# Attention over 32 heads: values two tiles at a time, six tiles of each head's softmax sum added by DMAs, the context normalised a head later

## What is computed

```python
xn = layernorm(x)
qkv = xn @ qkvw + qkvb                       # 32 heads of 32 columns each
scores = einsum('bhqd,bhkd->bhqk', q, k) / sqrt(32)
probs = softmax(scores)                      # rows of 2048 keys
ctx = einsum('bhqk,bhkd->bhqd', probs, v)
attn = ctx @ ow + ob
gate = softmax of the 16 best router scores of 64 experts, zero elsewhere
z = (xn @ A_w.T) * gate                      # 64 experts of rank 8
out = x + attn + (z @ B_w.T) * 2
```

## Time and profile before

| | |
|---|---|
| median of three runs | 2847.87 us |
| the profiled execution | 2850.67 us |
| its span in the trace | 2848.9 us |
| TensorE busy (matmul) | 2751.8 us, 97% |
| VectorE busy | 1637.0 us, 57% |
| ScalarE busy | 1289.9 us, 45% |
| GpSimd busy | 1733.5 us, 61% |
| mean granted TensorE clock | 0.98 |

### The profile page before, as it was taken

One profiled execution on the slowest core, in us unless ns is written; L12 is line 12 of the kernel. 1 busy time (PEld: TensorE's weight loads), 2 busy tenths in 40 slices (PEclk: granted clock), 3 DMA queues, 4 the chain that ended last, 5 costly groups with the idle time before them and its releaser, 6 DMA issues. The chain is left out here.

```text
span 2848.9 us, 36121 instructions
## 1 busy us (share of the span) xinstructions
PE 2751.8 (97%) x13776; PEld 1612.5 (57%) x13776; DVE 1637.0 (57%) x2553; ACT 1289.9 (45%) x2299; POOL 1733.5 (61%) x406
## 2 busy tenths in 40 slices
PE   7999999999799999999999999999999999997999
PEld 6888887778444444444444444444444444436887
DVE  8411111111778777777777778777877787724221
ACT  3111111110066666666666666666666666672100
POOL 0111111110199989898999899889989998982121
PEclk9999999999599999999999999999999999998999
DMA  4233333112611121112111211221122111004432
GB/s 140 98 129 112 110 110 111 66 66 89 162 27 38 38 60 34 38 38 60 35 41 35 60 35 42 45 50 38 38 51 44 38 38 35 9 16 144 128 103 92
DMA packets 145852, 188.56 MB, mean 66 GB/s; under 512 B 87152, under 2 KB 112240, under 8 KB 134896
## 3 DMA queue, kind: packets, MB, share of 16 engines
q1 hardware_dynamic: 145712, 186.70, 23.6%
HBM read 122.44 MB, written 63.69 MB: 65 GB/s over the span
## 5 line engine op out<-in xcount | busy, mean ns | idle before, releaser
L859 DVE TENSOR_REDUCE part_max<-ps_b 128x1 f32<-128x512 f32 x2048 | 1276.2, 682 | 399.8 <-PE ps_b L740 398.0
L706 POOL TENSOR_TENSOR psum_p<-psum_p,probs 128x2048 f32<-128x2048 f32 x316 | 1455.9, 4607 | 47.1 <-ACT probs L837 1.4
L837 ACT ACTIVATE probs<-ps_b 128x512 f32<-128x512 f32 x2048 | 1114.1, 597 | 743.7 <-PE ps_b L730 742.2
L730 PE MATMUL ps_b<-qp,kp 97*128 97x512 f32 x2048 | 880.4, 434 | 1.4 <-ACT probs L837 1.3
L740 PE MATMUL ps_b<-kp,qp 96*128 96x512 f32 x2048 | 765.7, 417 | 50.2 <-DVE part_max L859 35.6
L730 PEld LDWEIGHTS ps_b<-qp,kp 97*128 97x128 f32 x2048 | 386.3, 189 | 627.3 <-ACT probs L837 453.8
L758 PE MATMUL ps_b<-probs,vh 128*32 128x512 f32 x4096 | 556.5, 616 | 2.5
L740 PEld LDWEIGHTS ps_b<-kp,qp 96*128 96x128 f32 x2048 | 400.4, 196 | 146.7 <-DVE part_max L859 80.6
L232 POOL TENSOR_TENSOR wlo<-wraw,whi 128x1024 fp32r<-128x1024 f32 x29 | 69.5, 2397 | 612.7 <-ACT whi L335 612.7
L261 PE MATMUL ps_a<-xhi,whi 128*128 128x512 f32 (+1 forms) x928 | 370.7, 399 | 1.0 <-DVE elo L424 0.9
L261 PE MATMUL ps_a<-xlo,whi 128*128 128x512 f32 (+1 forms) x928 | 367.7, 396 | 0.0
(11 more groups left out here) (72 smaller groups left out, 1100.5 us busy)
## 6 DMA issues: line engine op xcount, KB each, us to landing
kp<-qk_scr SPq DMA_DIRECT2D x96, 256.0 KB, 4.1
qp<-qk_scr SPq DMA_DIRECT2D x96, 256.0 KB, 6.3
qk_scr<-ehi SPq DMA_DIRECT2D x16, 1024.0 KB, 3.9
qk_scr<-elo SPq DMA_DIRECT2D x16, 1024.0 KB, 6.7
wraw<-wcat SPq DMA_DIRECT2D x29, 512.5 KB, 7.5
craw<-cz_scr SPq DMA_DIRECT2D x16, 768.0 KB, 5.0
stage<-x SPq DMA_DIRECT2D x16, 512.0 KB, 4.4
v_scr<-elo SPq DMA_DIRECT2D x16, 512.0 KB, 3.3
```

The lines of the kernel that those rows point to most:

```text
L706: pool.tensor_tensor(acc[:, :], (acc if n else probs[0])[:, :], probs[t % RING][:, :], ALU.add) \
L730: pe.matmul(ps[:, st_bank(g, j, b), :], kp[j][0:PACK + 1, t * P:(t + 1) * P], qp[j][0:PACK + 1, b * NQ:(b + 1) * NQ], start=True, stop=Tru ...
L837: act.activation(probs[t % RING][:, b * NQ:(b + 1) * NQ], ps[:, st_bank(g, j, b), :], ACT.Exp, scale=SCALE).then_inc(exp_done, 1)
L859: dve.tensor_reduce(part_max[jn % 2][:, tn, b:b + 1], ps[:, MAX_BANK + bank, :], AX_X, ALU.max) \
```

## The change

- **Values.** `values` runs for two tiles at a time, at every even step from 2 on (tiles t-2 and t-1), and for tiles 14 and 15 at step 0 of the next head. Steps are no longer in halves.
- **Banks.** `scores_t` has three banks in rotation. The ring of four banks now also takes the sums and the transposed maxima; the sums' own bank is gone. `LEAD` is 4, `SLOTS` (buffers of q, k and v) 3.
- **Sums.** ScalarE writes the exps of tile 0 to one of two new tiles, `psum_q`, and not to the ring. Tiles 3, 6, 9, 12 and 14 are added onto it by DMAs that accumulate (`accum_op=ALU.add`), issued by GpSimd, 128x2048 each; each waits until the one before has landed. GpSimd adds the other ten tiles with 9 adds. TensorE multiplies `psum_q` and `psum_p` by ones at step 6 of the next head; it no longer multiplies single tiles by ones, but in the last head.
- **Normalising.** The context of head h is multiplied by its reciprocals in head h + 2, at steps 1 to 4, in four parts of 128 columns, each after the second maximum of its step. The reciprocal is taken at step 9. SP stores head h - 2 before it inverts the sums of head h - 1.
- The loops over groups of four heads become one loop over 32 heads. The last head has three `scores_t` banks, as all others.

The diff, cut to its core:

```diff
-POOL_TILES = [0, 1, 2, 3, 4, 6, 7, 8, 9, 11, 12, 14]
+BASE_TILE = 0
+CHAIN_TILES = [3, 6, 9, 12, 14]
+POOL_TILES = [1, 2, 4, 5, 7, 8, 10, 11, 13, 15]
+POOL_ORDER = [2, 3, 4, 5, 6, 7, 8, 9, 10, 11, 12, 13, 15, 14]
 LAST_POOL_TILES = [0, 1, 2, 3, 4, 6, 8, 10]
+LAST_ONES_TILES = [5, 7, 9, 11, 12, 13, 14, 15]
-LEAD = 3
-POOL_SUMS_AT, TAKE_SUMS_AT, RECIPROCAL_AT, NORMALISE_AT = 3, 4, 8, 10
-SLOTS = 4
+LEAD = 4
+SUMS_AT, RECIPROCAL_AT, NORMALISE_AT = 6, 9, 1
+SLOTS = 3
...
-        ST_BANKS, MAX_BANKS = 2, 4
-        MAX_BANK, PV_BANK, SUM_BANK = 2, 6, 7
+        ST_BANKS, RING_BANKS = 3, 4
+        RING_BANK, PV_BANK = 3, 7
...
         @block.gpsimd
+            def chain(h, t):
+                if t == CHAIN_TILES[0]:
+                    pool.wait_ge(pv_done, TT * h + BASE_TILE + 1)
+                wait(pool, chained, chain_count(h, t) - 16)
+                pool.wait_ge(exp_done, 64 * h + 4 * t + 4)
+                pool.sem_inc(cleared, 1)
+                pool.dma_start(psum_q[h % 2][:, :], tile(h, t)[:, :], accum_op=ALU.add).then_inc(chained, 16)
...
+                for t in POOL_ORDER:
+                    if t in CHAIN_TILES:
+                        chain(h, t)
+                    else:
+                        add(h, t)
...
         @block.tensor
+            def sums(h):
+                u = ("sum", h, 0, 0)
+                wait_ring(pe, u)
+                pe.wait_ge(chained, chain_count(h, CHAIN_TILES[-1]))
+                sum_of(ring_bank(u), psum_q[h % 2], True, False)
+                pe.wait_ge(pool_done, pool_count(h, POOL_TILES[-1]))
+                sum_of(ring_bank(u), psum_p[h % 2], False, True).then_inc(sum_ready, 1)
...
+            def step(h, t):
+                for b in range(QB):
+                    if h >= 0:
+                        scores_t(h, t, b)
+                    if has_maxima(h, t):
+                        scores(h, t, b)
+                if h < 0:
+                    return
+                if t == 0 and h >= 1:
+                    values(h - 1, TT - 2)
+                    values(h - 1, TT - 1)
+                if h < LAST:
+                    if t % 2 == 0 and t >= 2:
+                        values(h, t - 2)
+                        values(h, t - 1)
+                elif t >= 1:
+                    values(h, t - 1)
+                    if t - 1 in LAST_ONES_TILES:
+                        last_sums(t - 1)
+                if t == SUMS_AT and h >= 1:
+                    sums(h - 1)
...
         @block.vector
+                        if b == 1 and h >= 2 and 0 <= t - NORMALISE_AT < QB:
+                            normalise(h - 2, t - NORMALISE_AT)
```

More of the change, by code:

```diff
@@ L585, in target @@
[L585 to L618, removed]
+        def target(h, t):
+            return (h + 1, t + LEAD) if t + LEAD < TT else (h + 2, t + LEAD - TT)
@@ L620, in attend, with tile @@
+        def tile(h, t):
+            return psum_q[h % 2] if based(h, t) else probs[slot(h, t)]
+        previous = {}
+        held = {}
+        for h in range(HEADS):
+            for t in range(TT):
+                if not based(h, t):
+                    previous[h, t] = held.get(slot(h, t))
+                    held[slot(h, t)] = (h, t)
         block = ctx.enter_context(nc.Block())
@@ L761, in values @@
+                if not (h == LAST and t in LAST_ONES_TILES):
                     last.then_inc(pv_done, 1)
-            def sums(g, j, t):
-                mine = tiles(g, j)[1]
-                if t not in mine:
-                    return
-                if t == mine[0]:
-                    wait(pe, sums_taken, number(g, j))
-                for b in range(QB):
-                    last = pe.matmul(ps[b * HD:(b + 1) * HD, SUM_BANK, :], ones[:, :],
-                                     probs[t % RING][:, b * NQ:(b + 1) * NQ], start=(t == mine[0]), stop=False)
-                last.then_inc(pv_done, 1)
@@ new lines, in _ @@
+            for h in range(-1, HEADS):
+                if h >= 0:
+                    pe.wait_ge(negmax_loaded[h % SLOTS], 16 * (h // SLOTS + 1))
+                for t in range(first_step(h), TT):
+                    step(h, t)
+                    if t == TRANSPOSED_AT and h < LAST:
+                        transpose_max(h + 1)
+            values(LAST, TT - 1)
+            last_sums(TT - 1)
+            pe.wait_ge(pool_done, pool_count(LAST, LAST_POOL_TILES[-1]))
+            sum_of(ring_bank(("sum", LAST, 0, 0)), psum_p[LAST % 2], False, True).then_inc(sum_ready, 1)
@@ L918, in project_output @@
+                    if t == TRANSPOSED_AT and h < LAST:
+                        take_transposed(h + 1)
+            for part in range(QB):
+                normalise(LAST - 1, part)
+            dve.wait_ge(sum_ready, HEADS)
+            dve.wait_ge(ctx_ready, QB * LAST)
+            dve.reciprocal(recip_b[:, :], ps[:, ring_bank(("sum", LAST, 0, 0)), :]).then_inc(recip_done, 1)
+            for part in range(QB):
+                normalise(LAST, part)
 def project_output(nc, x, w2, bias, cz_scr, w_early, early_loaded, out):
```

398 lines of the change are left out of this document (197 added, 201 removed).

## The result

The changed kernel takes 2799.73 us, the median of four runs (2797.96 to 2805.34), against 2847.32 before: a ratio of 0.984, 95% interval 0.982 to 0.985. It is faster by 48 us, clear of the noise; 160 were forecast (2687), and the time is at the edge of the range (2610 to 2800). The profiled execution took 2805.3 us, its span is 2803.3.

What follows compares the result with a forecast made beforehand. TensorE sets the pace, GpSimd is next. Per head GpSimd 49.8 and TensorE 50.3, plus 0.5 for mutual waits: 50.8, 5.5 less than 56.3; 2850.7 - 170 + 6.5 = 2687 us, range 2610 to 2800.

Steps and rivals of the forecast that it cites:

- TensorE's own path: TensorE's work alone in a head, with paired values, fewer ones matmuls and the transposed maxima: 48.8 us.
- a visit: On TensorE, the changes of shape around one group of values matmuls: some 0.3 us each time.
- a DMA of the chain: One accumulating 1 MB DMA onto psum_q, costed as two transfers back to back: lands 7.1 us after its issue.
- So of 7 us some 1.5 reach TensorE, as much as the 1.41 of now: Of the four normalising parts' waits on VectorE, only 1.5 us a head was to hold up TensorE.
- The phase argument: Normalising parts at steps 1 to 4, placed against GpSimd's gap and adds: waits of about 1.5, 0, 2.3 and 3 us.
- Rival B: Parts meet GpSimd's adds at random, 8 us of waits, some 5 reaching TensorE: 54 us a head, 2786 us; chance 0.15.
- the order is free: On SP, storing head h - 2 before inverting the sums delays nothing: sums ready from step 6, row 97 wanted at 13.
- the 1.5 us of GpSimd's wait: Between tile 14's DMA and the next head's tile 3's lies one add, so GpSimd waits 1.5 us for the landing.
- The last head: With three score banks the fourth score waits for the first's exp, some 0.25 us a step: 4 us more.
- Rival C: Slower, the chain of accumulating DMAs is the bound: above 11.1 us each a head exceeds 56.3 us; at 13, 3152; chance 0.10.
- rival D: No gain: the pairs starve ScalarE and TensorE waits what it saves, about 2850 us; chance 0.03.
- A: Rival: all is hidden in GpSimd's gaps and TensorE alone sets 49.2 us a head, 2637 us; chance 0.17.

Runs made afterwards that it cites:

- The lock alone: Changed kernel, multiply still in four parts on VectorE, but each accumulating DMA adds only the first 1024 of 2048 columns: 2802.32 us (0.985).
- the best kernel: Changed kernel with the multiply on GpSimd, tile 15's sum on TensorE, four accumulating DMAs, four banks in the last head and LEAD 5: 2631.75 us (0.924).

## Why the prediction was wrong

- **Direction and what bounds the kernel: right.** TensorE's own path was forecast at 48.8 us a head and is 48.4; the pair 5.88 against 5.80; a visit 0.3 against 0.30; the issue 0.9 against 0.87 us; a DMA of the chain 7.1 against 7.6 in the median, all but tile 14's. But of 160 us forecast only 48 came.
- **The step that failed** is "So of 7 us some 1.5 reach TensorE, as much as the 1.41 of now". The sum of the parts was near (6.4 us, 5.4 of them waits, for 6.8 of waits); their shares were wrong. The phase argument gave waits of 1.5, 0, 2.3 and 3 us; they are 1.0, 3.8, 0.4 and 0.2, and the part forecast to wait for nothing waits for a whole add, with VectorE already behind. So 3.1 us a head of idle time reach TensorE in place of 1.5, and the half clock behind it, 5.7 us a head, costs some 2.7 more by the estimate above. The sum gave the clock no price, although had it. The lock alone costs 6.1 us a head (54.5 against 48.4). 54.6 for 50.8 is 3.8 us over 30 heads, 114 us: the miss.
- **Rival B** had 54 us a head and 2786, close to what came. Its number was in part luck: it had four waits at random, 8 us in all, where two at fixed places make 4.8 of 5.4, and some 5 us of idle time, where there are 3.1 and the clock. The rule of the Trainium skill on the shared port (SBUF — State Buffer, "Who interferes with whom"), by which the second to come is blocked until the first ends, was the better guide, and the trace agrees: 0.13 us from the add's start to the part's, 0.14 from end to end. B deserved more than 0.15, as its condition (adds for most of the time) stood in the sum.
- **A second step was wrong without being felt**: "the order is free" for SP, and the 1.5 us of GpSimd's wait. Nothing was costed for small DMAs that meet an accumulating one, nor for the chain meeting the loads: 1.5 us of wait became 5.2, as the DMA of tile 14 lands in 11.5 us and not in 7.1. In the changed kernel this costs TensorE nothing; without the lock it costs 4.0 us a head. Had the lock been as cheap as forecast, the time would have been about 2740 (an estimate from the 2737.98 of the multiply on GpSimd), still not 2687. GpSimd's adds (4.7 us each) and issues held.
- **The last head** was to cost 4 us and cost 9.2 (49.8 against 40.7), the one wait counted, its echo on ScalarE not. The fourth bank brings back 8.5 of the 9.2.
- **The first heads** were better than said: the first copy came 5.7 us earlier, where 2.5 us more were forecast for LEAD, as head 0 has the gain of a head without parts.
- Rival C did not happen (7.6 us, not 11.1); rival D neither. A's 49.2 us a head is met by the best kernel (49.04), once both costs are taken out, but by chance: that kernel has a fifth less of the chain and one more tile of ones on TensorE.

## What to carry to other kernels

Before an operation is cut into parts, ask what each part must wait for: here a part of a quarter of the size waited as long as the add lasted, and engines that wait for the same event meet in the same way in nearly every round. Look at the phase in the trace before you count on it. Price the clock of a stall with the stall. An accumulating DMA is not only as long as it takes to land: look for every small DMA on the path that sets the end, and for the loads, and place the big ones where neither is under way. And take out costs one at a time and together: the second may be hidden by the first, and then neither removal alone shows what both give. Here removing the lock gave 2.2 us a head, shortening the DMAs alone nothing, and both 6.2.

## What was not expected of the hardware

- In the kernel with the multiply on GpSimd, an 8 KB DMA of SP that met an accumulating 1 MB DMA landed 0.16 to 0.21 us after it in 26 of 30 cases; its median went from 1.8 to 5.4 us.
- An accumulating 1 MB DMA between SBUF tiles lands 7.0 us after its issue at the least, 7.6 in the median of the changed kernel and up to 12.4 beside 1.8 MB of loads; half of it takes 4.6 in the median.
- VectorE's reciprocal takes 0.94 us for 128x128 and 3.34 for 128x512, where a multiply of the same size takes 0.27 and 0.69 when GpSimd adds nothing: it is no stand-in for one.
